# Column sums by one VectorE reduction and new shares of weight preparation in a two-layer conditional feed-forward kernel

## The chip, the cores and the metric

The kernel runs on one core of a Trainium2 chip. The metric is the device time of one execution in microseconds (us). A core has five engines with queues of their own that meet at semaphores: TensorE (PE, matrix products into PSUM), VectorE (DVE), ScalarE (ACT), GpSimd (POOL, which does not touch PSUM here) and SyncE (SP, which issues nearly all transfers). Each engine runs its instructions in the order in which they are written.

## The reference, cut to what matters

`x` is 32 x 64 x 1024 in fp32. Two layers follow one another, each with a residual:

```
x = x + ffn0(cond0(x));   x = x + ffn1(cond1(x))
cond(x)[b] = W[itok[b]]^T x[b]              # 64 x 64 matrix chosen by sample, contracts the channels
ffn0(y) = y @ (ternary(w) * scale) + b      # ternary(w) = 0 if |w| < 0.05 else sign(w)
          scale[o] = mean over k of |w[k, o]|
ffn1(y) = y @ dequant(q).T + bias + 4 * (y @ A.T) @ B.T
          dequant(q) = NF4_LEVELS[q] * q_scale (one scale for 64 values), A and B of rank 8
```

Everything is fp32. The scale of the first feed-forward is a column sum of absolute weights; it multiplies the product's columns.

## The kernel before, in words

**Tiles.** The 32 samples are 16 tiles (g = 0 to 15) of 128 rows and 1024 columns. Layer 1 takes the same tiles again as g = 16 to 31, in pairs. The 1024 output columns are two halves n of 512 (one PSUM bank each). TensorE's products use operands split in a high part (rounded to fp32r, by ScalarE) and a low part (the difference, by VectorE): `high_x` and `low_x` do this for the mixed input.

**Layer 0.** `mixed` or, from tile 4 (F = 4) on, `mixed_batches(g)` (L1159) applies the sample's 64 x 64 matrix on TensorE and leaves the transposed result in PSUM; ScalarE and VectorE split it. `mixed_batches(g)` waits for `low_x(g - 1)` (L1166), and the first of them, tile 4, waits for both `colscale` (L1164), since they read the same PSUM tile. `first` (tiles 0 to 3) and `main` (from tile 4 on) are sixteen matmuls each for one tile and one half against the ternary weights T0. VectorE's `leave_y(q)` (L936) multiplies the product by `col_scale` into `ys`, and GpSimd adds bias (`add_bias`, L600) and result (`result_half`, `result`) to x.

**Column sums.** ScalarE turns the sixteen weight blocks in `w_in` (8 row blocks k, two halves n) into absolute values (`absolute`, semaphore s_abs) after VectorE or ScalarE has made signs for `ternary`. GpSimd's `sums(n, 1, KB)` (L621) adds the eight blocks of a half in seven additions into `col_scale`; both halves are at the head of GpSimd's queue (L669, L670). `column_sums(n)` (L1273) adds over the partitions on TensorE with a matrix of ones; `column_sums(1)` stands in the middle of `first(1, 1)` (L1321). ScalarE's `colscale(n)` (L738) copies the sum out of PSUM divided by 1024. `leave_y(4)` is the first to need the second half.

**The weights of layer 1** are prepared during layer 0, in 16 pieces d of 128 x 512. For each piece ScalarE makes 8 lines of the integer levels (`lines`, L743), VectorE joins them by 6 maxima (`maxima`, L944), GpSimd takes the difference and scales it (`weight`), TensorE turns it and adds the LoRA part (`turn_w(d)`, L1289), and ScalarE and VectorE split it or make block sums of it (`high_w`, `low_w`, `keep_block`, `sums_with`), which depends on the rest of d by 4. At the end `high_sums` and `low_sums` split those sums.

**Stages.** The order is written out by stages m = 0 to 31. On VectorE and ScalarE stage m = 2g + n belongs to tile g and half n; for tiles 0 to 3 the eight stages lie behind the ternary weights, each with a share of the maxima and, at even m, one `leave_y(3 + g)`; from m = 8 on each starts with `leave_y(m - 1)`, then the operations on a piece turned in the stage before, then `low_x` of the next tile (even m), then the maxima. `low_x(4)` comes at the end of stage 6. `share(total, m)` (L196) says how much of a total is done before stage m: weight 3 for each of the first 8 stages, 10 for the next 21, the last three none. This gives 9 of the 96 maxima in the first eight stages, 4 or 5 in each of the others. `lines_by` makes the lines go some ahead, `ready_in(d)` (L212) is the stage that completes piece d's maxima, `turned_in(d)` (L216) is two later, but not before stage 8. ScalarE calls `colscale(1)` ahead of stage 2 (L874). SyncE loads the levels of a piece (`load_q`, L503, three buffers) when the lines of the piece three before are done, in the order of the loop at L560, ahead of spills and loads of x. In stages 29 to 31 `SPLIT_BY` (L185) puts 4, 5 and 1 of the late splits.

**Layer 1** works with pairs of tiles and seven products of half size for each pair; its right sides are the prepared weights.

Of the kernel before, what the change touches and what calls it, by code (L numbers as in the profile page):

```python
# [30 lines left out]
ALU = mybir.AluOpType  # L31
# [3 lines left out]
BANK = 512  # L35
# [66 lines left out]
def build(nc, x, itok, mix0, w0, b0, mix1, q_weight, q_scale, b1, lora_a, lora_b, out):  # L102
# [14 lines left out]
    B, C, T = x.shape  # L117
# [3 lines left out]
    NT = B * C // P  # L121
    KB = T // P
    NH = T // BANK
# [10 lines left out]
    F = 4  # L134
# [20 lines left out]
    ABS = ((2, 3, 0, 1, 5, 4, 7, 6), (0, 1, 2, 3, 4, 5, 6, 7))  # L155
# [36 lines left out]
    def stays(g):  # L192

        return SB <= g < SB + XS

    def share(total, m):  # L196


        m = min(m, NH * NT - 3)
        whole = 3 * NH * F + 10 * (NH * (NT - F) - 3)  # L200
        return total * (3 * min(m, NH * F) + 10 * max(0, m - NH * F)) // whole

    def lines_by(m):

# [7 lines left out]
    def ready_in(d):  # L212

        return next(m for m in range(NH * NT) if share(2 * NC * ND, m + 1) >= 2 * NC * (d + 1))

    def turned_in(d):  # L216

        return max(NH * F, ready_in(d) + 2)

    def blocks_before(d):  # L220

# [11 lines left out]
    with ExitStack() as ctx:  # L233
# [6 lines left out]
        def sem(name):  # L240
            return ctx.enter_context(nc.semaphore(name))
# [8 lines left out]
        col_scale = sb("col_scale", [P, T], F32)  # L250
# [42 lines left out]
        def w_raw(k, n):  # L293
            return w_in[:, k, n * BANK:(n + 1) * BANK]
# [100 lines left out]
        s_neg = sem("s_neg")  # L395
        s_T0 = sem("s_T0")
        s_sum = sem("s_sum")
        s_colsum = sem("s_colsum")
        s_colscale = sem("s_colscale")
        s_ah = sem("s_ah")  # L400
# [82 lines left out]
        def _(sp):  # L483
# [76 lines left out]
            for g in range(F, NT):  # L560
                load_mix(g + 3)
                for d in range(3, ND):
                    if d > 3 and ready_in(d - 3) // NH == g or d == 3 and g == F:
                        load_q(d)
                if g == F:
                    for t in range(F):
                        spill(t)
                else:
                    if g == NT - 1:
                        sp.wait_ge(s_xb, NT)  # L570
                        sp.dma_start(bias[:, :], b1.rearrange("(a f) -> a f", a=1).to_broadcast([P, T])
                                     ).then_inc(s_b1, 16)
                    if g - 1 < NT - XS:
                        spill(g - 1)
                    if g + 3 < NT:
                        load_x(g + 3)
# [21 lines left out]
        @block.gpsimd  # L598
        def _(pool):
            def add_bias(g):  # L600
                arrived(pool, g)
                pool.wait_ge(s_b1 if g >= NT else s_b0, 16)
                pool.wait_ge(s_xT, NH * (g + 1))
                pool.tensor_tensor(x_of(g), x_of(g), bias[:, :], ALU.add  # L604
                                   ).then_inc(s_xb, 1)

            def result_half(q):
                t, n = q % F, q // F
                pool.wait_ge(s_xb, t + 1)
                pool.wait_ge(s_ys, q + 1)  # L610
                pool.tensor_tensor(half(t, n), half(t, n), ys[:, t, :], ALU.add).then_inc(s_res0, 1)  # L611

            def result(g):
                pool.wait_ge(s_xb, g + 1)
                pool.wait_ge(s_ys, NH * (g + 1))
                at = NH * g % F
                pool.tensor_tensor(x_of(g), x_of(g),  # L617
                                   ys[:, at:at + NH, :].rearrange("p a f -> p (a f)"), ALU.add
                                   ).then_inc(s_res0, NH)

            def sums(n, start, stop):  # L621

                cols = slice(n * BANK, (n + 1) * BANK)
                for j in range(start, stop):
                    pool.wait_ge(s_abs, n * KB + j + 1)
                    if j == 1:
                        pool.tensor_tensor(col_scale[:, cols], w_raw(ABS[n][0], n), w_raw(ABS[n][1], n),
                                           ALU.add).then_inc(s_sum, 1)
                    else:
                        pool.wait_ge(s_sum, n * (KB - 1) + j - 1)  # L630
                        pool.tensor_tensor(col_scale[:, cols], col_scale[:, cols],  # L631
                                           w_raw(ABS[n][j], n), ALU.add).then_inc(s_sum, 1)

            def weight(d):
                k, n = PIECES[d]
                lev = side_p[:, d % SP, :]
                pool.wait_ge(s_max, 2 * NC * (d + 1))
                pool.tensor_tensor(lev, lev, side_n[:, :], ALU.subtract).then_inc(s_lev, 1)  # L638
                pool.wait_ge(s_lev, d + 1)
                sc = scales[:, n * HB:(n + 1) * HB, 2 * k:2 * k + 2].unsqueeze(3).to_broadcast(  # L640
                    [P, HB, 2, P // 2])
                lev4 = lev.rearrange("p (o g i) -> p o g i", o=HB, g=2)
                pool.tensor_tensor(lev4, lev4, sc, ALU.mult).then_inc(s_wn, 1)

            def weights_of(m):
                for d in range(ND):
                    if ready_in(d) == m:
                        weight(d)

            def low_side(p, i):  # L650

                o = (S1, S2, S3, S4)[i - 1]
                pool.wait_ge(s_sideh, NPR * p + o + 1)
                pool.tensor_tensor(side(o, 1).rearrange("p b c -> p (b c)"), plain(i),  # L654
                                   side(o, 0).rearrange("p b c -> p (b c)").bitcast(F32), ALU.subtract
                                   ).then_inc(s_Sl, 1)

            def add_sum(p, i):
                which, tile, n = SUMS[i]
                pool.wait_ge(s_xb, SB + 2 * p + tile + 1)  # L660
                pool.wait_ge(s_take, taken(p, 2 + which))
                t = half(SB + 2 * p + tile, n)
                pool.tensor_tensor(t, t, sum_of(which), ALU.add).then_inc(s_sum2, 1)  # L663

            pool.memset(ident[:, :], 0.0).then_inc(s_zero, 1)
            pool.wait_ge(s_zero, 1)
            pool.affine_select(out=ident[:, :], in_=ident[:, :], compare_op=ALU.not_equal, fill=1.0,
                               base=0, pattern=[[-1, P]], channel_multiplier=1).then_inc(s_ident, 1)
            sums(0, 1, KB)  # L669
            sums(1, 1, KB)  # L670
            add_bias(0)
            result_half(0)
            add_bias(1)
            result_half(1)
            pool.wait_ge(s_scales, 16)
            add_bias(2)
            result_half(2)
            for m in range(NH * F - 3):
                weights_of(m)
            add_bias(3)  # L680
            result_half(3)
            result_half(F)
            add_bias(F)
            result_half(F + 1)
            for m in range(NH * F - 3, NH * F + 1):
                weights_of(m)
            result_half(F + 2)
            for g in range(F, SB):
                if g == F:
                    result_half(F + 3)  # L690
                else:
                    result(g - 1)
                if g > F:
                    weights_of(NH * g)
                add_bias(g + 1)
                weights_of(NH * g + 1)
            for i in range(1, 5):
                low_side(0, i)
            result(NT - 1)
            add_bias(SB + 1)  # L700
            for p in range(NP):
                for i in range(len(SUMS)):
                    add_sum(p, i)
                if p + 1 < NP:
                    add_bias(SB + 2 * p + 2)
                    low_side(p + 1, 1)
                    low_side(p + 1, 2)
                    add_bias(SB + 2 * p + 3)
                    low_side(p + 1, 3)
                    low_side(p + 1, 4)  # L710

        @block.scalar
        def _(act):
# [157 lines left out]
            act.wait_ge(s_ain, 64)  # L871
            act.activation(loraA[:, :], a_raw, ACT.Copy).then_inc(s_ah, 1)
            for g in range(SB):
                if g == 1:  # L874
                    colscale(1)
                for m in (NH * g, NH * g + 1):
                    for d in range(ND):
# [31 lines left out]
        def _(dve):  # L909
# [169 lines left out]
            leave_y(1)  # L1079
            for k in range(4, KB):  # L1080
                ternary(1, k)
            dve.wait_ge(s_ah, 1)
            dve.tensor_tensor(loraA[64:P, :], a_raw[64:P, :], loraA[64:P, :].bitcast(F32),
                              ALU.subtract).then_inc(s_al, 1)
# [46 lines left out]
        def _(pe):  # L1131
# [139 lines left out]
                mm.then_inc(s_prod, 1)  # L1271

            def column_sums(n):  # L1273
                pe.wait_ge(s_sum, (n + 1) * (KB - 1))
                pe.wait_ge(s_fill, 3)
                pe.wait_ge(s_hl, NH * 3)
                pe.matmul(flat(n), ones[:, :], col_scale[:, n * BANK:(n + 1) * BANK],
                          start=True, stop=True).then_inc(s_colsum, 1)
# [88 lines left out]
```

## Time and profile before

| | us |
|---|---|
| median of 3 runs | 343.64 |
| lowest and highest | 343.38, 344.93 |
| profiled execution, its time | 344.56 |
| its span | 342.5 |
| PE busy | 332.4 (97%) |
| POOL busy | 245.0 (72%) |
| DVE busy | 236.0 (69%) |
| ACT busy | 164.5 (48%) |

The span runs from the first to the last instruction; the time of the execution has 2.1 us more around it. The clock granted to TensorE was 0.999 of full speed. A row of the timeline gives the start, the duration, the engine and the line of the kernel, the instruction, the tile written and the tile read, their shapes, how many rows were merged, and in brackets how long the engine was idle before it and what ended that.

### The profile page before, as it was taken

The numbers are of one execution on the slowest core, as the hardware profiler recorded it, in microseconds if no ns is written. First come the engines' busy times: TensorE is split into PE (matmuls) and PEld (weight loads), VectorE is DVE, ScalarE is ACT, GpSimd is POOL, SyncE is SP. The second block draws the span as 40 slices with busy tenths as digits, with TensorE's granted clock in tenths as the row PEclk, the third lists the DMA queues.
The fourth block names the chain that finished last, engine by engine and source line by source line (L and its number), as shares of the span: only waits on it lengthen the run. The fifth ranks groups of instructions, "written<-read, shape, count | busy, mean of one in ns | idle before, by whom it ended". The sixth has DMA issues, their size and how long they took to land.

```text
span 342.5 us, 8187 instructions
## 1 busy us (share of the span) xinstructions
PE 332.4 (97%) x3142; PEld 271.4 (79%) x3142; DVE 236.0 (69%) x356; ACT 164.5 (48%) x300; POOL 245.0 (72%) x160
## 2 busy tenths in 40 slices
PE   7999999989999999999799999999999999999996
PEld 6868778778888778887678888888888888888884
DVE  7787567899999999999999736346263462624623
ACT  1799357877897787788171403214032140411400
POOL 0298999998896896986578966766467664677642
PEclk9999999999999999999999999999999999999999
DMA  6894511644354245300100151412513124150302
GB/s 229 291 341 132 201 33 33 271 168 159 118 167 162 93 157 177 141 10 13 55 2 3 65 189 63 150 44 74 181 65 131 63 84 169 67 169 23 124 31 92
DMA packets 25800, 40.60 MB, mean 119 GB/s; under 512 B 7810, under 2 KB 16002, under 8 KB 25762
## 3 DMA queue, kind: packets, MB, share of 16 engines
q1 hardware_dynamic: 25090, 39.48, 33.3%
q10 hardware_dynamic: 672, 0.61, 0.5%
q8 instruction: 25, 0.41, 0.5%
q14 instruction: 13, 0.11, 0.1%
HBM read 25.40 MB, written 14.68 MB: 117 GB/s over the span
## 4 chain that ended last, share of the span: by engine, by line
PE 51%; DVE 20%; POOL 12%; issue 8%; ACT 4%; DMA 1%; SPq 1%; DVEq 0%; POOLq 0%; ACTq 0%
PE acc L1268 45%; POOL col_scale L631 4%; DVE hl L914 3%; DVE ys L941 3%; POOL x_first L604 3%; PE spare L1154 2%; PE xT L1154 2%; POOL x_first L611 2%; DVE side_n L953 2%; ACT spare L762 2%; DVE W L988 2%; DMA w_in<-in_L_ffn_w 1%; POOL side_p L638 1%; DVE side_p L953 1%; DVE side_n L956 1%
## 5 line engine op out<-in xcount | busy, mean ns | idle before, releaser
L1268 PE MATMUL acc<-W,hh 128*128 128x512 f32 x256 | 81.4, 389 | 0.0
L1228 PE MATMUL acc<-T,hh 128*128 128x512 f32 x192 | 76.5, 398 | 0.0
L1228 PE MATMUL acc<-T,hl 128*128 128x512 f32 x192 | 75.0, 391 | 0.0
L604 POOL TENSOR_TENSOR X<-X,bias 128x1024 f32<-128x1024 f32 x28 | 68.1, 2432 | 0.0
L762 ACT ACTIVATE spare<-q_raw 128x512 f32<-128x512 int32 x96 | 56.1, 599 | 20.2 <-DVE side_n L953 5.0
L1040 DVE TENSOR_TENSOR X<-X,acc 128x512 f32<-128x512 f32 x48 | 32.9, 685 | 36.7 <-PE acc L1268 28.9
L1268 PEld LDWEIGHTS acc<-W,hh 128*128 128x128 f32 x256 | 48.0, 188 | 10.0
L663 POOL TENSOR_TENSOR X<-X,ys 128x512 f32<-128x512 f32 x24 | 30.5, 1299 | 34.1 <-DVE ys L1029 34.1
L1268 PE MATMUL acc<-W,hl 128*128 128x512 f32 x128 | 49.8, 389 | 0.0
L797 ACT ACTIVATE hh<-xT 128x512 fp32r<-128x512 f32 x16 | 8.7, 595 | 77.6 <-PE xT L1154 77.6
L1228 PEld LDWEIGHTS acc<-T,hh 128*128 128x128 f32 x192 | 36.0, 188 | 8.0
L1228 PEld LDWEIGHTS acc<-T,hl 128*128 128x128 f32 x192 | 36.1, 188 | 7.3
L1029 DVE TENSOR_TENSOR ys<-acc,ys 128x512 f32<-128x512 f32 x16 | 11.0, 690 | 34.2 <-PE acc L1268 33.3
L617 POOL TENSOR_TENSOR X<-X,ys 128x1024 f32<-128x1024 f32 x12 | 29.3, 2438 | 2.8 <-DVE ys L941 2.7
L638 POOL TENSOR_TENSOR side_p<-side_p,side_n 128x512 f32<-128x512 f32 x16 | 20.8, 1299 | 13.4 <-DVE side_n L959 13.4
L1268 PEld LDWEIGHTS acc<-W,hl 128*128 128x128 f32 x128 | 24.0, 188 | 5.0
L654 POOL TENSOR_TENSOR side_S<-plain_sums,side_S 128x512 fp32r<-128x512 f32 x8 | 10.4, 1302 | 23.0 <-ACT side_S L814 23.0
L941 DVE TENSOR_TENSOR ys<-acc,col_scale 128x512 f32<-128x512 f32 x32 | 21.8, 683 | 3.7 <-POOL x_first L611 3.7
L1268 PE MATMUL acc<-W 128*128 128x512 f32 x96 | 24.0, 399 | 0.0
L1268 PE MATMUL acc<-W,side_S 128*128 128x512 f32 x96 | 23.2, 390 | 0.0
L1268 PE MATMUL acc<-W_T,W 128*128 128x512 f32 x96 | 23.1, 389 | 0.0
L654 POOL TENSOR_TENSOR hl<-plain_sums,hh 128x512 fp32r<-128x512 f32 x16 | 21.6, 1353 | 0.0
(98 smaller groups left out, 606.5 us busy)
## 6 DMA issues: line engine op xcount, KB each, us to landing
out<-X SPq DMA_DIRECT2D x22, 512.0 KB, 3.1
X<-in_x SPq DMA_DIRECT2D x12, 512.0 KB, 3.4
X<-out SPq DMA_DIRECT2D x12, 512.0 KB, 3.8
q_raw<-in_L_ffn_q_weight SPq DMA_DIRECT2D x16, 256.0 KB, 2.9
w_in<-in_L_ffn_w SPq DMA_DIRECT2D x14, 256.0 KB, 6.8
x_first<-in_x SPq DMA_DIRECT2D x4, 512.0 KB, 5.1
out<-x_first SPq DMA_DIRECT2D x4, 512.0 KB, 4.6
out<-X SPq DMA_DIRECT2D x4, 256.0 KB, 2.0
```

The source lines that it names most:

```text
L604: pool.tensor_tensor(x_of(g), x_of(g), bias[:, :], ALU.add).then_inc(s_xb, 1)
L617: pool.tensor_tensor(x_of(g), x_of(g), ys[:, at:at + NH, :].rearrange("p a f -> p (a f)"), ALU.add).then_inc(s_res0, NH)
L631: pool.tensor_tensor(col_scale[:, cols], col_scale[:, cols], w_raw(ABS[n][j], n), ALU.add).then_inc(s_sum, 1)
L638: pool.tensor_tensor(lev, lev, side_n[:, :], ALU.subtract).then_inc(s_lev, 1)
L654: pool.tensor_tensor(side(o, 1).rearrange("p b c -> p (b c)"), plain(i), side(o, 0).rearrange("p b c -> p (b c)").bitcast(F32), ALU.subtra ...
L663: pool.tensor_tensor(t, t, sum_of(which), ALU.add).then_inc(s_sum2, 1)
L762: act.activation(dst, q_raw[:, d % QS, :, :].rearrange("p o i -> p (o i)"), ACT.Copy, scale=slope, bias=offset).then_inc(s_line, 1)
L941: dve.tensor_tensor(ys[:, q % F, :], acc[:, bank_of(q), :], col_scale[:, n * BANK:(n + 1) * BANK], ALU.mult).then_inc(s_ys, 1)
L1040: dve.tensor_tensor(t, t, bank, ALU.add).then_inc(s_take, 1)
L1154: mm = pe.matmul(turned(g, h)[c * C:(c + 1) * C, k, rows], x_of(g)[rows, at:at + C], mix[rows, g % NM, rows], start=True, stop=True)
L1228: mm = pe.matmul(acc[:, bank_of(q), :], a[:, k, :], T0[:, n, k, :], start=(k == 0 and j == 0), stop=(k == KB - 1 and j == 1))
L1268: mm = pe.matmul(acc[:, bank, :], a[:, k, :], w1(part, c, k), start=(k == 0 and j == 0), stop=(k == HB - 1 and j == len(terms) - 1))
```

## The change

It touches the column sums of the second half and the spread of the weight preparation over the stages.

- The second half's eight absolute blocks are summed by one `tensor_reduce` on VectorE, behind the last `ternary(1, k)` and ahead of the loraA difference, in place of seven additions on GpSimd. `column_sums(1)` waits for it (s_reduce).
- `share` uses a list of weights: 5 for each of the first eight stages, 10 for the next 18, 6 for the last three. The maxima of the stages become 2 in each of the first eight (16 in all), 4 in each of stages 8 to 25, then 3, 2 and 3. They were 1, 1, 1, 1, 2, 1, 1, 1 and then 4, with 5 in stages 9, 19 and 28.
- `turned_in(d)` is at least stage 8 + d. The stages in which pieces 0 to 15 are turned become 8, 9, 10, 11, 13, 14, 16, 17, 19, 20, 22, 23, 25, 26, 28, 30. They were 8, 10, 11, 13, 14, 16, 17, 19, 20, 22, 23, 25, 26, 28, 29, 30.
- ScalarE calls `colscale(1)` ahead of stage 4 instead of stage 2.
- On GpSimd `add_bias(2)` and `add_bias(3)` come ahead of the results that stood before them.
- `load_q(d)` follows the new stages; for tile 4's turn of SyncE's loop it is pieces 3 to 6.

```
+    SHARES = [5] * (NH * F) + [10] * 18 + [6] * 3
     def share(total, m):
-        m = min(m, NH * NT - 3)
-        whole = 3 * NH * F + 10 * (NH * (NT - F) - 3)
-        return total * (3 * min(m, NH * F) + 10 * max(0, m - NH * F)) // whole
+        return total * sum(SHARES[:m]) // sum(SHARES)
...
     def turned_in(d):
-        return max(NH * F, ready_in(d) + 2)
+        return max(NH * F + d, ready_in(d) + 2)
...
                 for d in range(3, ND):
-                    if d > 3 and ready_in(d - 3) // NH == g or d == 3 and g == F:
+                    if max(F, ready_in(d - 3) // NH) == g:
                         load_q(d)
...
-            sums(0, 1, KB)
-            sums(1, 1, KB)
+            sums()
             add_bias(0)
             result_half(0)
             add_bias(1)
             result_half(1)
+            add_bias(2)
             pool.wait_ge(s_scales, 16)
-            add_bias(2)
+            add_bias(3)
             result_half(2)
             for m in range(NH * F - 3):
                 weights_of(m)
-            add_bias(3)
             result_half(3)
...
             for g in range(SB):
-                if g == 1:
+                if g == 2:
                     colscale(1)
...
             for k in range(4, KB):
                 ternary(1, k)
+            dve.wait_ge(s_abs, NH * KB)
+            dve.tensor_reduce(col_scale[:, BANK:T], w_in[:, :, BANK:T].rearrange("p k f -> p f k"),
+                              mybir.AxisListType.X, ALU.add).then_inc(s_reduce, 1)
...
             def column_sums(n):
-                pe.wait_ge(s_sum, (n + 1) * (KB - 1))
+                if n == 0:
+                    pe.wait_ge(s_sum, KB - 1)
+                else:
+                    pe.wait_ge(s_reduce, 1)
```

## Rows read from the trace of the kernel before

**Rows 1.** The page's first part: busy us, share of the span, instructions.

```profile
PE 332.4 (97%) x3142; PEld 271.4 (79%) x3142; DVE 236.0 (69%) x356; ACT 164.5 (48%) x300; POOL 245.0 (72%) x160
```

**Rows 2.** Timeline of PE, opening: start, us, line, operation, tiles, idle before.

```profile
38.52 1.02 PE L1277 MATMUL xT<-col_scale,ones 128*128 128x512 f32 x2
...
44.96 1.16 PE L1172 MATMUL xT<-mix,X 64*64 64x64 f32 x64
46.05 3.92 PE L1216 MATMUL acc<-T,h 128*128 128x512 f32 x16
49.90 1.16 PE L1172 MATMUL xT<-mix,X 64*64 64x64 f32 x64
```

**Rows 3.** Timeline of PE, from tile 5 on: mixings and the last piece.

```profile
70.21 1.16 PE L1172 MATMUL xT<-mix,X 64*64 64x64 f32 x64
...
79.46 1.16 PE L1172 MATMUL xT<-mix,X 64*64 64x64 f32 x64
...
88.75 1.16 PE L1172 MATMUL xT<-mix,X 64*64 64x64 f32 x64
...
98.78 1.16 PE L1172 MATMUL xT<-mix,X 64*64 64x64 f32 x64
...
157.63 1.48 PE L1154 MATMUL xT<-mix,X 64*64 64x64 f32 x64
164.82 0.63 PE L1296 MATMUL acc<-ident,side_p 128*128 128x128 f32 x4 [1.86 <-DVE W_sums L978]
...
165.61 1.48 PE L1154 MATMUL spare<-mix,X 64*64 64x64 f32 x64
```

**Rows 4.** Groups of instructions: the piece turned; busy us, mean ns, idle before.

```profile
L1296 PE MATMUL acc<-ident,side_p 128*128 128x128 f32 x64 | 9.7, 274 | 3.5 <-DVE W_sums L978 1.9 <-DVE W_sums L974 1.3 <-DVE W_sums L981 0.3
```

**Rows 5.** Busy time by stretch: PE, PEld, DVE, ACT, POOL, clock, DMA.

```profile
70.00:155.00 85.00, 84.23 (x916) 68.28 (x915) 80.10 (x128) 68.50 (x129) 70.42 (x42) 1.00 0.40 135
```

**Rows 6.** Timeline of DVE, opening and the late splits.

```profile
32.19 0.69 DVE L932 SCALAR_TENSOR_TENSOR T<-w_in,spare 128x512 fp32r<-128x512 f32 x1 [0.46 <-ACT w_in L736]
33.14 1.25 DVE L1083 TENSOR_TENSOR loraA<-a_in,loraA 64x1024 fp32r<-64x1024 f32 x1 [0.26 <-ACT loraA L872]
34.43 0.69 DVE L941 TENSOR_TENSOR ys<-acc,col_scale 128x512 f32<-128x512 f32 x1
35.03 0.68 DVE L953 SCALAR_TENSOR_TENSOR side_p<-side_p,spare 128x512 f32<-128x512 f32 x1
...
40.70 0.69 DVE L959 TENSOR_TENSOR side_p<-side_p,spare 128x512 f32<-128x512 f32 x1 [3.80 <-ACT spare L762]
...
41.91 0.68 DVE L953 SCALAR_TENSOR_TENSOR side_n<-side_n,spare 128x512 f32<-128x512 f32 x1
42.69 0.69 DVE L956 SCALAR_TENSOR_TENSOR side_n<-side_n,spare 128x512 f32<-128x512 f32 x1
...
46.81 1.29 DVE L914 TENSOR_TENSOR hl<-xT,hh 128x512 fp32r<-128x512 f32 x2 [0.65 <-ACT hh L720]
...
52.95 0.69 DVE L941 TENSOR_TENSOR ys<-acc,col_scale 128x512 f32<-128x512 f32 x1 [3.66 <-POOL x_first L611]
...
156.62 5.66 DVE L988 TENSOR_TENSOR W<-W_sums,W 128x512 fp32r<-128x512 f32 x4
```

**Rows 7.** Timeline of ACT: the second half's scale.

```profile
39.58 0.60 ACT L740 ACTIVATE col_scale<-xT 128x512 f32<-128x512 f32 x1 [4.94 <-PE xT L1277]
```

**Rows 8.** Timeline of POOL: six of the second half's adds.

```profile
26.25 9.30 POOL L631 TENSOR_TENSOR col_scale<-col_scale,w_in 128x512 f32<-128x512 f32 x6
```

**Rows 9.** Groups of VectorE instructions near to the new one; busy us, mean ns.

```profile
L941 DVE TENSOR_TENSOR ys<-acc,col_scale 128x512 f32<-128x512 f32 x32 | 21.8, 683 | 3.7 <-POOL x_first L611 3.7
...
L1083 DVE TENSOR_TENSOR loraA<-a_in,loraA 64x1024 fp32r<-64x1024 f32 x1 | 1.3, 1252 | 0.3 <-ACT loraA L872 0.3
...
L1044 DVE MEMSET b_wide<- 128x1024 f32 x1 | 0.9, 912 | 0.2 <-issue 0.2
...
L1058 DVE CAST loraB<-acc 128x512 fp32r<-128x512 f32 x2 | 2.1, 1117 | 1.2 <-PE acc L1284 1.2
```

More of the change, by code:

```diff
@@ L397, in build @@
         s_sum = sem("s_sum")
+        s_reduce = sem("s_reduce")
         s_colsum = sem("s_colsum")
@@ L619, in result, with sums @@
                                    ).then_inc(s_res0, NH)
[L621 to L625, printed above, removed]
+            def sums():
+                cols = slice(0, BANK)
+                for j in range(1, KB):
+                    pool.wait_ge(s_abs, j + 1)
                     if j == 1:
-                        pool.tensor_tensor(col_scale[:, cols], w_raw(ABS[n][0], n), w_raw(ABS[n][1], n),
+                        pool.tensor_tensor(col_scale[:, cols], w_raw(ABS[0][0], 0), w_raw(ABS[0][1], 0),
                                            ALU.add).then_inc(s_sum, 1)
                     else:
-                        pool.wait_ge(s_sum, n * (KB - 1) + j - 1)
+                        pool.wait_ge(s_sum, j - 1)
                         pool.tensor_tensor(col_scale[:, cols], col_scale[:, cols],
-                                           w_raw(ABS[n][j], n), ALU.add).then_inc(s_sum, 1)
+                                           w_raw(ABS[0][j], 0), ALU.add).then_inc(s_sum, 1)
             def weight(d):
```

## The prediction

> **What bounds the kernel now.** The engine shares come first [rows 1]: TensorE is busy for 332.4 of 342.5 us, so the time is TensorE's work plus the few places where it waits, and another engine counts only where it makes TensorE wait. Next I read TensorE in order of time through layer 0. In the opening [rows 2] the column sums of the second half start at 38.52, the mixing of tile 4 at 44.96 and that of tile 5 at 49.90 with no wait between. From tile 5 on [rows 3] a tile with one turned weight piece takes 9.25 us (70.21 to 79.46) and one with two 10.03 (88.75 to 98.78). The eleven tiles from 49.90 to 157.63 have fifteen pieces: 11 x 8.47 + 15 x 0.78 = 104.9 us, and take 107.7, so 2.8 us are lost. From 157.63 to 165.61 there is one mixing (1.48), one `main` (3.7) and one piece (0.8), 6.0 of 8.0 us: 2.0 more. Of these 4.8 us the rows show 3.5 as waits before a piece is turned, ended by VectorE's weight sums [rows 4]; the largest, 1.86, is at 164.82 [rows 3]. The rest are short waits of the queue and matmuls that are slower just behind one. The stretch behind 185 us is not touched by the change.
>
> From 70 to 155 us VectorE is as full as TensorE (80.1 of 85 us [rows 5], and what is missing is the start of one operation behind another). But in the opening it idles [rows 6]: 3.80 us at 40.70, because ScalarE, standing in `colscale(1)` until 39.58 [rows 7], made no lines, 0.65 at 46.81, and 3.66 at 52.95, because GpSimd was late with `result_half`.
>
> **The change part by part.** *The adds that go.* Seven GpSimd adds go, six of which take 9.30 us from 26.25 [rows 8]. TensorE did not wait for them: the sums were out at 35.55 and the matmul came at 38.52 [rows 2]. What follows on GpSimd starts up to 10 us earlier, once the bias has landed, and the 3.66 us of VectorE at 52.95 go, as the result it waited for is then early. None of this is on TensorE's path by itself.
>
> *The reduction.* The trace has no such instruction. It reads 8 x 512 elements per partition, neighbours of the sum 4 KB apart, at one output in eight reads. From below: a memset of 1024 elements, which reads nothing, takes 0.912 us [rows 9], so 4096 are put at no less than 3.65. Packed operations that read: 1.252 us for 1024 against 0.683 for 512, a slope of 1.11 ns, gives 0.683 + 3584 x 1.11 ns = 4.7 us. The only VectorE operation here with far apart elements is the cast at L1058, which writes with a step of 32 bytes: 1.117 us where a packed one takes 0.683, so 0.85 ns more for each element [rows 9]. With that for the reads: 4.7 + 4096 x 0.85 ns = 8.1 us. From above: 8 x 1.117 = 8.9 us. I take 8.1, since far apart elements are what the two have in common and the only ones measured cost it, and keep 3.65 and 8.9 for the range.
>
> The Trainium skill is of two minds on this. Its page "SBUF — State Buffer" (section "Door 1: The DMA port swizzle") says that full rate wants at least two accesses in each 16-byte line and that a new line at every access costs extra; the cast bears it out for writes, no row here shows it for reads. Its page "VectorE: DVE Perf Modes" (section "Mode 1× (REGULAR) — the baseline") says that the plain mode gives one result a cycle whatever the stride; with its formula of (N + 151) cycles at 0.96 GHz that would be an estimated 4.4 us. The second is the first rival below.
>
> *The path through the opening.* The last `ternary` starts at 32.19 [rows 6] and the next instruction can follow 0.60 later, so the reduction runs 32.8 to 40.9. `column_sums(1)` on TensorE, in order at 38.52, waits for it: 2.4 us. VectorE's queue behind the reduction is the loraA difference (1.29), `leave_y(2)` (0.6), then maxima and `leave_y` in order; one follows another after 0.60, or 0.78 where it needs the one before [rows 6]. The new shares put two maxima in each of the first eight stages (16 in all) where there were nine. ScalarE now takes `colscale(1)` only after the lines of four stages, eleven of them, and the eleventh must wait for the sixth maximum, which is done at 47.7 (42.2 for `leave_y(2)`, then two maxima, `leave_y(3)`, four maxima). A line and `colscale(1)`, 0.6 each, end at 48.9. `mixed_batches(4)` waits for that: 48.9 for 44.96, 3.9 late in all. `leave_y(4)` starts at 48.9 too.
>
> *Tile 5.* `mixed_batches(5)` waits for `low_x(4)`. Before, eight maxima stood in front of it on VectorE, and it was done at 48.1, 1.8 us before TensorE came for it [rows 2, 6]. Now 14 do: from 48.9 come `leave_y(4)`, four maxima, `leave_y(5)`, four maxima, then the two `low_x`: 6 x 0.60 + 4 x 0.78 + 1.29 = 8.0 us (ScalarE's copies for it, some 0.6 us each, are hidden: they can start 6.0 in, when the line behind the twelfth maximum is made). It is done at 56.9. TensorE comes at 48.9 + 4.94 = 53.8 and waits 3.1. So `mixed_batches(5)` is at 56.9 for 49.90: **7.0 us late**. What the six early maxima and the reduction fill of VectorE's idle time is in this sum already.
>
> *What comes back.* From stage 26 on the maxima are 3, 2 and 3 for 4, 4 and 5, and with stage 24 and the piece operations VectorE has seven operations fewer (some 4.6 us) before the late `low_sums`, which took 5.66 us in one block at 156.62 [rows 6] and stood in front of the two sums that TensorE waited for at 164.82. Piece 14 is turned at stage 28 instead of 29, so its sums now come ahead of that block. The 2.0 us there and the wait of that kind before 157.63 go. In the middle a close pair remains: old, pieces with rest 1 and 2 were turned in neighbouring stages (10/11, 16/17, 22/23, 28/29) with one sum between; new, rest 2 and 3 are (10/11, 16/17, 22/23), with three VectorE operations between. For the first pair, counted from `mixed_batches(5)`: TensorE is there after 1.1 + 3.75 + 0.75 + 3.7 + 0.75 + 1.1 + 3.7 + 0.75 + 3.7 = 19.3 us; VectorE has two `leave_y` and two maxima (2.5), `low_x(5)` (to 3.7), four maxima (6.7), `leave_y`, `low_w` and four maxima (11.2), `leave_y`, a sum and `low_x(6)` (14.2), four maxima (17.2), and `leave_y` with the three (19.7). I leave 0.4 us for this and 0.4 for the other two, where the two engines go at one rate. Of 4.8 us lost, **4.0 come back**; the bounds are none and all.
>
> *Other edits.* `add_bias` and the `s_scales` wait swap on GpSimd, with slack. SyncE's `load_q` moves with the shares, and its fourth now stands before the spills of tiles 0 to 3 and waits for 32 lines; `load_x(8)` now stands behind the lines of stage 11, a whole tile before its own is mixed. Nothing on the path: the stretch of TensorE between covers it, and if it didn't, the transfer would be late once, by the part that sticks out, some 1 us.
>
> *Sum.* 7.0 - 4.0 = +3.0 us. The profiled execution has a span of 342.5 us and a time of 344.56, 0.9 above the median; against itself it becomes 347.6, and the median of 343.64 becomes **346.6 us**.
>
> **Rivals.** *A: the reduction runs at the packed rate, 4.7 us.* It ends at 37.5, before TensorE comes to the column sums. All steps are 3.4 us earlier: `low_x(4)` at 53.5, 3.6 late, 4.0 back: -0.4, so 343.2 us. For it: it is one input stream, and no read in the trace shows a stride cost. Against it: the cast.
>
> *B: faster.* The reduction goes at the rate of a memset (3.65) and every later wait vanishes: `low_x(4)` at 52.5, 2.6 late, 4.8 back, -2.2, so 341.4 us. It is one mechanism, VectorE's idle 8.1 us of the opening used for work that the late stages then lack, and it decides from where `low_x(4)` comes before about 53.0 (reduction under 4.2 us). Against it: 14 maxima are in front.
>
> *C: the shares bring nothing back.* If the late waits come from the order of the pieces and `low_sums` rather than from the number of maxima, the 7.0 us stay whole: 350.6 us (347.2 with the packed rate). For it: TensorE and VectorE go at one rate, so a stage cannot catch up. Against it: the two sums do move ahead of the block.
>
> **How the numbers follow.** Forecast 0.55, A 0.28, B 0.08, C 0.09. Within 0.5% (1.7 us) is about what a measurement of this kernel can tell from no change. The forecast's own range is 345.4 to 348.2 (reduction 7.3 to 8.9, 3.2 to 4.3 back); nearly all of it is slower. A lies within 0.5% in three of four cases and splits the rest. So faster 0.12, same 0.24, slower 0.64. The range reaches down into A's lower side and up to the forecast's upper end: 342.2 to 348.3, leaving out B and most of C.
>
> **What would show it.** The first row to look at is the reduction's duration: 8 us or 4.5. Then `column_sums(1)` (40.9 or 38.5), `mixed_batches(4)` (48.9 or 45.5) and `mixed_batches(5)` (56.9 or 53.5); the wait before the second mixing names `low_x(4)` on VectorE. Then the distance from `mixed_batches(5)` to the first `mixed_alone`, 107.7 before and some 105.7 after, and no wait before the piece after it. I am wrong in the opening if the maxima in front of `low_x(4)` cost less than 0.60 each or ScalarE does not hold `colscale(1)` back; wrong in the middle if that distance does not shrink.

## The result and the profile after

| | us |
|---|---|
| before, median of 4 runs | 343.8 (343.38 to 344.93) |
| after, median of 4 runs | 349.53 (347.33 to 351.10) |
| ratio, 95% interval | 1.015 (1.0096 to 1.0204) |
| profiled execution after: time, span, granted clock | 347.33, 345.3, 0.995 |

The change makes the kernel slower by 1.5%. The forecast was 346.6 with a range to 348.3. The profiled execution is the fastest of the four; the others have spans of 347.5, 347.5 and 349.3 at clocks of 0.995, 0.994 and 0.990. The kernel before had 0.999 in its profile. Beside the experiments it ran 79 times: 58 executions had 0.998 to 1.000, and 21 had 0.994 or 0.995 and were 0.9 us longer in the mean. So there are two questions: where the profiled execution's +2.8 us of span come from, and what the others lose besides.

The page's first part, after:

```profile
PE 331.6 (96%) x3142; PEld 270.7 (78%) x3142; DVE 244.3 (71%) x357; ACT 164.8 (48%) x300; POOL 234.8 (68%) x153
```

VectorE has 8.3 us more and GpSimd 10.2 less [rows 1]: the one instruction more, the seven less. Below, "mixing 4" and "mixing 5" are `mixed_batches(4)` and `mixed_batches(5)`. Timeline of VectorE: the reduction, `leave_y(4)` and `low_x(4)`.

```profile
32.38 7.53 DVE L1084 TENSOR_REDUCE col_scale<-w_in 128x512 f32<-128x4096 f32 x1
...
48.30 0.69 DVE L942 TENSOR_TENSOR ys<-acc,col_scale 128x512 f32<-128x512 f32 x1 [1.24 <-ACT col_scale L741]
...
55.27 1.28 DVE L915 TENSOR_TENSOR hl<-xT,hh 128x512 fp32r<-128x512 f32 x2
```

Timeline of TensorE: the rows that answer to [rows 2, 3], L1284 the column sums, L1176 a mixing, L1220 `first`, L1158 `mixed_alone`, L1272 a product of layer 1.

```profile
39.96 1.12 PE L1284 MATMUL xT<-col_scale,ones 128*128 128x512 f32 x2 [1.73 <-DVE col_scale L1084]
48.35 1.16 PE L1176 MATMUL xT<-mix,X 64*64 64x64 f32 x64 [1.80 <-ACT col_scale L741]
49.44 5.53 PE L1220 MATMUL acc<-T,h 128*128 128x512 f32 x16
56.70 1.16 PE L1176 MATMUL xT<-mix,X 64*64 64x64 f32 x64 [1.72 <-DVE hl L915]
61.56 0.60 PE L1303 MATMUL acc<-ident,side_p 128*128 128x128 f32 x4
...
161.63 1.48 PE L1158 MATMUL xT<-mix,X 64*64 64x64 f32 x64
166.85 0.60 PE L1303 MATMUL acc<-ident,side_p 128*128 128x128 f32 x4
167.61 1.48 PE L1158 MATMUL spare<-mix,X 64*64 64x64 f32 x64
...
179.13 3.01 PE L1272 MATMUL acc<-W,side_S 128*128 128x512 f32 x12 [0.73 <-DVE ys L942]
187.51 0.69 PE L1158 MATMUL xT<-mix,X 64*64 64x64 f32 x32
```

Three waits stand in the opening where there were none. Mixing 5 is at 56.70 for 49.90, 6.8 us late: the three waits are 5.25 us, and `first(3, 1)` between the last two takes 5.53 us where it took 3.92 [rows 2]. From there to the first `mixed_alone` it is 104.93 us for 107.73, and on to the second 5.98 for 7.98: all 4.8 us of [rows 3, 4] are gone. From there to the next pair it is 19.90 for 19.11, a new loss of 0.8. Sum: 6.8 - 2.8 - 2.0 + 0.8 = +2.8 us, the difference of the spans.

The new 0.8 us: product 3 waits for `leave_y(31)`, behind five `low_sums` that take 6.60 us where they took 4.90. First the kernel after (VectorE, then GpSimd), then the kernel before. (The bracket at 165.93 names a transfer, but the addition starts 0.2 us behind the end of VectorE's `leave_y`, as the one at 163.05 does.)

```profile
166.88 6.60 DVE L989 TENSOR_TENSOR W<-W_sums,W 128x512 fp32r<-128x512 f32 x5
165.93 2.38 POOL L619 TENSOR_TENSOR X<-X,ys 128x1024 f32<-128x1024 f32 x1 [3.12 <-DMA bias<-in_L_ffn_bias]
168.28 2.84 POOL L606 TENSOR_TENSOR X<-X,bias 128x1024 f32<-128x1024 f32 x1
```

```profile
165.79 4.90 DVE L988 TENSOR_TENSOR W<-W_sums,W 128x512 fp32r<-128x512 f32 x5
163.05 2.36 POOL L617 TENSOR_TENSOR X<-X,ys 128x1024 f32<-128x1024 f32 x1 [1.93 <-DVE ys L941]
165.37 2.37 POOL L604 TENSOR_TENSOR X<-X,bias 128x1024 f32<-128x1024 f32 x1
```

After, one GpSimd addition from SBUF begins inside the block and runs along with it; before, the last one ends 1.95 us into it. That fits the Trainium skill, page "SBUF — State Buffer", section "Who interferes with whom": a VectorE instruction with two inputs in SBUF contends with GpSimd reads, a `tensor_reduce` does not. On the `tensor_reduce` the trace agrees: GpSimd's result addition at 32.96, beside the reduction, took 1.30 us as elsewhere. The 0.8 us come with the new shares and not with the reduction: shares_only, which has no reduction, has the block of 6.60 us and a wait of 0.73 there, and reduce_only, with the old shares, has 4.88 and no wait. That the second GpSimd addition is what lengthens the block was not tested by itself; `three_adds` below shows the two engines' additions slowed side by side.

### The profile page after: what moved, and what is told of

Its sections match the earlier page's. It is cut to its first block, busy times and chain, and to the rows that moved or that the text cites. A ratio compares the mean times of both kernels' runs of the same rounds, so it can differ in the third digit from the quotient of the medians.

```text
span 345.3 us, 8175 instructions
## 1 busy us (share of the span) xinstructions
PE 331.6 (96%) x3142; PEld 270.7 (78%) x3142; DVE 244.3 (71%) x357; ACT 164.8 (48%) x300; POOL 234.8 (68%) x153
## 4 chain that ended last, share of the span: by engine, by line
PE 77%; DVE 8%; issue 6%; ACT 6%; SPq 1%; DMA 1%; DVEq 0%; ACTq 0%
PE acc L1272 43%; PE acc L1232 23%; PE xT L1176 3%; PE xT L1158 2%; PE acc L1303 2%; PE spare L1158 2%; ACT spare L731 2%; ACT w_in L737 2%; DVE W L989 1%; DMA w_in<-in_L_ffn_w 1%; PE acc L1305 1%; DVE ys L942 1%; ACT spare L763 1%; DVE T L933 1%; DVE side_p L954 1%
## 5 line engine op out<-in xcount | busy, mean ns | idle before, releaser
L1272 PE MATMUL acc<-W,hh 128*128 128x512 f32 x256 | 81.4, 389 | 0.0
L1272 PEld LDWEIGHTS acc<-W,hh 128*128 128x128 f32 x256 | 48.1, 188 | 10.0
L1272 PE MATMUL acc<-W,hl 128*128 128x512 f32 x128 | 49.8, 389 | 0.0
L1272 PEld LDWEIGHTS acc<-W,hl 128*128 128x128 f32 x128 | 24.0, 188 | 5.0
L1272 PE MATMUL acc<-W 128*128 128x512 f32 x96 | 24.0, 399 | 0.0
L1272 PE MATMUL acc<-W,side_S 128*128 128x512 f32 x96 | 23.2, 390 | 0.7 <-DVE ys L942 0.7
L1272 PE MATMUL acc<-W_T,W 128*128 128x512 f32 x96 | 23.1, 389 | 0.0
L1272 PEld LDWEIGHTS acc<-W,side_S 128*128 128x128 f32 x96 | 17.9, 188 | 4.8 <-DVE ys L942 1.1
```

The source lines that it names most:

```text
L1272: mm = pe.matmul(acc[:, bank, :], a[:, k, :], w1(part, c, k), start=(k == 0 and j == 0), stop=(k == HB - 1 and j == len(terms) - 1))
```

## Experiments

Theories: **T**, the account above. **K**, the waits that TensorE now has in the opening make its granted clock fall from 2.4 to 1.2 GHz behind them; where that stretch lies ahead of another wait it is hidden, otherwise it adds to the time. The rivals are in the expectations. The kernel before ran again beside each group of experiments (14 or 17 executions, medians 343.9 to 344.6), and the ratios are to those.

| kernel | median us (lowest to highest) | ratio to before, 95% interval | clock of the profile |
|---|---|---|---|
| after_again | 348.98 (347.76 to 350.44) | 1.0119 (1.0089 to 1.0150) | 0.990 |
| shares_only | 349.00 (348.78 to 349.82) | 1.0140 (1.0112 to 1.0167) | 0.990 |
| reduce_only | 345.52 (344.66 to 346.61) | 1.0031 (1.0015 to 1.0048) | 0.995 |
| packed_reads | 346.56 (346.54 to 347.75) | 1.0069 (1.0046 to 1.0092) | 0.995 |
| filled_waits | 347.33 (346.95 to 347.63) | 1.0081 (1.0053 to 1.0110) | 0.999 |
| early_three | 346.98 (346.60 to 347.43) | 1.0072 (1.0051 to 1.0094) | 0.994 |
| colscale_early | 348.09 (347.86 to 348.71) | 1.0110 (1.0080 to 1.0140) | 0.990 |
| weight0_early | 345.89 (345.22 to 346.14) | 1.0040 (1.0026 to 1.0054) | 1.000 |
| balanced | 345.41 (344.76 to 346.51) | 1.0035 (1.0021 to 1.0050) | 1.000 |
| three_adds | 349.91 (349.48 to 352.32) | 1.0189 (1.0152 to 1.0226) | 0.989 |
| balanced_second | 344.07 (341.97 to 344.64) | 0.9991 (0.9973 to 1.0009) | 0.995 |
| balanced_third | 345.42 (342.84 to 346.85) | 1.0024 (1.0003 to 1.0045) | 0.995 |

**after_again**: no edit.

> The changed kernel once more, for its spread and a second profile. Theory T (the opening): mixed_batches(5) is late by some 7 us and 4 to 5 us come back later, so +3 us; that alone gives 346.7 to 347.3 in every execution. Theory K (the clock): the changed kernel's new waits of TensorE in the opening make the granted clock fall to half for some us behind them, and where that stretch lies beside TensorE's next wait it is hidden (as in the profile, +3), elsewhere it costs 2 us and more: executions differ, between 347 and 351 us, with the mean granted clock at 0.990 to 0.995, while the kernel before stays at 343.4 to 345 and 0.999.

Its profile is of its longest execution (span 348.4 for 345.3). Mixing 5 is at 56.46, as in the other profile, but the piece after it is turned 7.62 us later for 4.86. TensorE, and the granted clock by stretch (third column from the right):

```profile
56.46 1.99 PE L1176 MATMUL xT<-mix,X 64*64 64x64 f32 x64 [3.32 <-DVE hl L915]
64.08 0.60 PE L1303 MATMUL acc<-ident,side_p 128*128 128x128 f32 x4
...
56.00:58.00 2.00, 1.54 (x57) 1.57 (x61) 1.73 (x4) 1.12 (x2) 1.64 (x2) 0.50 0.00 0
58.00:60.00 2.00, 2.00 (x23) 1.59 (x16) 1.93 (x4) 1.50 (x4) 0.00 (x0) 0.50 0.00 0
60.00:62.00 2.00, 2.00 (x7) 1.52 (x6) 1.90 (x4) 1.81 (x5) 0.11 (x1) 0.50 0.12 35
```

In the first profile the clock fell a wait earlier (the same view of the kernel after):

```profile
50.00:52.00 2.00, 2.00 (x6) 1.62 (x5) 1.78 (x4) 1.80 (x4) 2.00 (x3) 0.50 0.00 0
52.00:54.00 2.00, 2.00 (x8) 1.55 (x7) 1.90 (x4) 1.76 (x4) 2.00 (x1) 0.76 0.11 33
...
56.00:58.00 2.00, 1.30 (x65) 1.27 (x66) 1.74 (x3) 1.24 (x4) 1.87 (x2) 1.00 0.00 0
```

There it lengthened `first(3, 1)` from 3.92 to 5.53 us, and as TensorE had to wait for `low_x(4)` until 56.7 anyway, that cost nothing. It is the same program with the same `low_x(4)` to wait for, and the piece is 2.5 us later by the clock alone. The other 0.6 us between the two spans lie behind 190 us and were not traced to a cause.

**filled_waits**:

```
+            keep_busy(flat(1), 7)        # 7 matmuls T0 x T0, nobody reads them
             column_sums(1)
...
+            pe.wait_ge(s_ys, 4)
+            keep_busy(acc[:, 3, :], 7)
             mixed_batches(F)
             first(3, 1, 0)
             first(3, 1, 1)
             pe.wait_ge(s_al, 1)
+            pe.wait_ge(s_ys, 5)
+            keep_busy(acc[:, 0, :], 14)
```

> The changed kernel with 7, 7 and 14 matmuls of 0.23 us, whose results nobody reads, put where TensorE waits in the opening (ahead of the second column sums, of mixing 4 and of mixing 5). Theory K (the clock falls behind an idle TensorE): the granted clock stays at 1.0 throughout, a piece is turned 4.9 us after mixing 5 in each execution, the time is 347.0 to 347.8 with a spread under 1.5 us, 1.5 to 2 us below the changed kernel's median, although TensorE does more. Rival R (the clock falls in these executions for another reason, or the spread comes from elsewhere): the median stays at 349 or goes up by what the matmuls overrun the waits.

As K says: TensorE gets 28 matmuls more, mixing 5 stays where it was, the clock of the four executions is 0.998 to 1.000, the spread 0.7 us, and the median 1.7 to 2.2 us below the changed kernel's two (1.3 to 2.4 by the ratios). Of the changed kernel's eight executions only the profiled one, 347.33, is as short as these four (346.95 to 347.63). What is left, 2.9 us above the kernel before beside it, is T's sum.

```profile
56.72 1.16 PE L1176 MATMUL xT<-mix,X 64*64 64x64 f32 x64 [0.17 <-DVE hl L915]
40.00:60.00 20.00, 19.60 (x201) 15.55 (x202) 17.08 (x27) 14.05 (x26) 12.08 (x9) 1.00 0.10 28
```

**packed_reads**:

```
-w_in[:, :, BANK:T].rearrange("p k f -> p f k")
+w_in[:, 0:HB, :].rearrange("p k (f j) -> p (k f) j", j=KB)
```

> The changed kernel with the reduction reading 4096 elements in a row (blocks 0 to 3, eight neighbours for each sum) instead of elements 4 KB apart; so the second half's scale is that of other elements. If the stride is what costs, the reduction takes 4.4 to 4.7 us instead of 7.5, the column sums no longer wait, low_x(4) is 3 us earlier and mixed_batches(5) near 53.6; theory T then gives 343.5 to 344.5 us. If the reduction is slow by itself, it takes 7.5 us again and the time is that of the changed kernel. Theory K: with one wait fewer in the opening the spread of the executions shrinks.

The reduction takes 4.41 us for as many elements, 4096, so the stride of 4 KB costs 3.1 us, 0.76 ns an element; no other stride was run. TensorE no longer waits for the sums, and mixing 5 is 2.7 us earlier. It still waits 3.32 there and the clock falls behind that: the piece is turned 6.47 us after mixing 5 for 4.86, so 1.6 of the 2.6 us by which 346.6 misses 344 are the clock's.

```profile
32.33 4.41 DVE L1084 TENSOR_REDUCE col_scale<-w_in 128x512 f32<-128x4096 f32 x1
```

```profile
54.03 1.16 PE L1176 MATMUL xT<-mix,X 64*64 64x64 f32 x64 [3.32 <-DVE hl L915]
```

**reduce_only**: the old shares (`[3] * 8 + [10] * 21`), stages, colscale(1) ahead of stage 2 and GpSimd's old order, with the reduction.

> The kernel before with the reduction alone on VectorE; shares, stages, the place of colscale(1) and GpSimd's order of biases as before. Theory T: the column sums are 1.5 us late (40.0 for 38.5), low_x(4) comes near 50 with eight maxima in front, mixed_batches(5) is near 51.4, and the later waits (4.8 us) stay, so +1.5 us: 345.2 us. Theory K adds what the clock takes behind the wait for the column sums: up to 349. Rival S: if only the shares were at fault, this is 343.8.

Mixing 5 is at 51.27, without a wait, and the late waits are back: 345.5, 0.9 above the kernel before beside it, where T said +1.5. The clock falls at the late wait, which the kernel before has too [rows 3], where the clock stayed at 1.00 in its profile:

```profile
165.75 0.63 PE L1303 MATMUL acc<-ident,side_p 128*128 128x128 f32 x4 [1.85 <-DVE W_sums L979]
165.00:190.00 25.00, 24.16 (x277) 19.88 (x278) 24.16 (x30) 9.37 (x18) 17.61 (x10) 0.93 0.01 2
```

**shares_only**: the reverse, the changed kernel with GpSimd's seven adds.

> The changed kernel with the second half summed by GpSimd as before (seven adds); shares, turned stages, ScalarE's later colscale(1) and the order of SyncE stay. Theory T: without the reduction (7.5 us) VectorE gets through its 14 maxima in time, leave_y(4) near 40.2 and low_x(4) near 48.2, so mixed_batches(5) stays at 49.9 and all 4.8 us of the later waits come back: 339 us (338.5 to 340.5), no fall of the clock. Rival S (the larger early shares are what is too much): low_x(4) is still late by 2 us or more, 341 to 343 us. Rival P: GpSimd, again late with the results, gives part of the later waits back: 341 to 342.

T's number was wrong by 10 us. `leave_y(4)` came at 40.2 as expected, but the tenth of the maxima then had to wait for 7.4 us: ScalarE's line of piece 1 waited for GpSimd's subtraction on piece 0, which stood behind four biases and three results.

```profile
49.34 0.63 ACT L763 ACTIVATE side_n<-q_raw 128x512 f32<-128x512 int32 x1 [7.20 <-POOL side_p L639]
42.07 4.75 POOL L605 TENSOR_TENSOR x_first<-x_first,bias 128x1024 f32<-128x1024 f32 x2
46.76 1.31 POOL L612 TENSOR_TENSOR x_first<-x_first,ys 128x512 f32<-128x512 f32 x1
48.00 1.31 POOL L639 TENSOR_TENSOR side_p<-side_p,side_n 128x512 f32<-128x512 f32 x1
55.90 1.98 PE L1173 MATMUL xT<-mix,X 64*64 64x64 f32 x64 [6.83 <-DVE hl L915]
```

So with the larger early shares GpSimd must either be rid of the second half's sums, as in the change, or take piece 0 earlier, as the last four kernels do: balanced_second keeps the sums on GpSimd and has mixing 5 at 49.69.

**early_three**: `SHARES = [3] * 8 + [10] * 18 + [6] * 3`.

> The changed kernel with weight 3 instead of 5 for the first eight stages (10 maxima there instead of 16; some 4.3 in the middle stages), all else kept: the reduction, the light last stages, the late colscale(1). Theory T2 (the reduction of 7.5 us and the six early maxima together overfill VectorE ahead of low_x(4); each alone is mostly absorbed): mixing 5 is near 51.4, with no wait in front of it, the later waits are gone as in the changed kernel, 341.5 to 342.5 us, clock at 1.0. Rival: the light stages can't be had without the early shares; then the later waits return in part, 343 to 345.

A miss, on both counts. Mixing 5 is at 53.05 and not at 51.4. In this profile the clock fell behind the 2.39 us wait for the sums, so TensorE came there just as `low_x(4)` was done; but `low_x(4)` is done only at 52.90 whatever the clock, as VectorE waited 1.24 us for the late `colscale(1)` at `leave_y(4)`. So the fall cost little here, and the four executions with a clock of 1.000 are at 346.6 to 347.2 beside 347.43. And the maxima saved in the opening return in the middle stages (4.3 each), and so do the waits. VectorE's `low_x(4)`, then TensorE:

```profile
51.62 1.28 DVE L915 TENSOR_TENSOR hl<-xT,hh 128x512 fp32r<-128x512 f32 x2
```

```profile
91.23 0.63 PE L1303 MATMUL acc<-ident,side_p 128*128 128x128 f32 x4 [0.31 <-DVE W L966]
121.09 0.63 PE L1303 MATMUL acc<-ident,side_p 128*128 128x128 f32 x4 [1.17 <-DVE W L966]
141.68 0.63 PE L1303 MATMUL acc<-ident,side_p 128*128 128x128 f32 x4 [1.15 <-DVE W_sums L982]
```

The rival holds: light last stages need the early shares. Its 343 to 345 us were too low, as it too had the opening at 51.4.

**colscale_early**: `if g == 1: colscale(1)`.

> The changed kernel with ScalarE's colscale(1) ahead of stage 2 again. Theory T2: mixing 4 no longer waits for it (46.4 instead of 48.2), but mixing 5 waits for low_x(4) all the same, which comes at 56.5 less at most 1.2 us (VectorE's wait of 1.24 at leave_y(4)): mixing 5 at 55.3 to 56.5, with a longer wait in front of it, and by theory K a longer stretch of half clock behind it. 348 to 350 us. Rival: if the place of colscale(1) is what delays the opening, mixing 5 is near 52 and the time near 344.

Mixing 4 is at 45.84 without a wait; mixing 5 waits 3.91 us and is at 54.77, 1.7 us earlier than in after_again: 1.24 are VectorE's wait at `leave_y(4)`, which is gone, and 0.4 an earlier start of the reduction (31.73 for 32.14). The clock falls behind it. 348.1 us: `low_x(4)` sets the opening.

**three_adds**: the reduction as three packed additions (4, 2, 1 blocks).

> The changed kernel with the reduction replaced by three packed VectorE additions (four blocks to four, two to two, one to one: 2048, 1024 and 512 elements). If the stride is what makes the reduction slow, the three take 2.3 + 1.2 + 0.7 = 4.2 us, or up to 5.5 where a GpSimd addition holds the port that two inputs from SBUF need, and the kernel goes as packed_reads did: 346 to 347 us. If VectorE's additions are slowed more by GpSimd, 348 or more.

They run from 31.65 to 39.5, as long as the reduction, where 4.2 us were expected of them alone. GpSimd's additions beside them are slowed as well: a result takes 3.22 us for 1.3. VectorE, then GpSimd:

```profile
31.65 5.07 DVE L1087 TENSOR_TENSOR w_in<-w_in 128x2048 f32<-128x2048 f32 x2
36.76 2.73 DVE L1087 TENSOR_TENSOR col_scale<-w_in 128x512 f32<-128x512 f32 x1
32.42 3.22 POOL L613 TENSOR_TENSOR x_first<-x_first,ys 128x512 f32<-128x512 f32 x1
35.60 6.09 POOL L606 TENSOR_TENSOR x_first<-x_first,bias 128x1024 f32<-128x1024 f32 x2
```

This is the last rival of the expectation, 348 us or more: packed additions with two inputs are no way round the stride while GpSimd adds beside them. The clock fell twice in this profile, behind waits of 2.04 and 2.22 us.

**Attempts at a faster kernel.** weight0_early is shares_only with GpSimd's `weight(0)` behind result 0 and `weight(1)` behind result 4.

> The kernel with new shares and GpSimd's seven adds (shares_only), but with GpSimd's work on piece 0 put behind the first result instead of behind the third, since there ScalarE's lines of piece 1 waited 7.2 us for it. Theory Q (in shares_only GpSimd's queue, not the number of maxima, made low_x(4) late): low_x(4) is done near 48, mixing 5 at 49 to 50 without a wait, all later waits are gone, clock at 1.0: 339.5 to 341 us, faster than both kernels. Rival S (14 maxima are too many in any case): low_x(4) near 52, 343 us. Rival: GpSimd is late at leave_y(7) and mixing 6 waits, 342.

Mixing 5 waits only 1.18 us and all waits from 75 to 165 are gone, but the first piece waits 2.59 for `leave_y(7)`, and two later ones 0.65 and 0.52. At 345.9 theory Q is right on what held shares_only up and wrong on the amount by 5 us. balanced adds `SHARES = [9] * 8 + [20] * 18 + [18, 14, 14]`.

> The column sums with GpSimd as before; GpSimd's work on piece 0 behind the first result, on piece 1 behind the fifth; colscale(1) ahead of stage 4; shares 9 for the first eight stages, 20 for the next 18, then 18, 14, 14 (14 maxima in the first eight stages, 12 of them ahead of low_x(4), exactly 4 in each middle stage, 4, 3, 3 at the end; piece 14 turned at stage 28). Theory Q (the opening is bounded by VectorE's and GpSimd's queues together, the late waits by the maxima in stages 26 to 28): low_x(4) is done by 49.6, mixing 5 comes without a wait, GpSimd has leave_y(7) released by 53.6, just before the first piece is turned; 2 us and more of the later waits are gone: 340.5 to 342.5 us, clock 1.0, faster than before. Rival: GpSimd still holds leave_y(7) or piece 1 back, and the opening loses 2 to 3 us: 343 to 344.5.

The rival: GpSimd stood waiting for piece 0's maxima, result 1 came late, and VectorE waited for it 4.22 us. balanced_second puts `weight(0)` behind result 1 and `weight(1)` behind result 3.

> The kernel balanced with GpSimd's work on piece 0 one result later (behind result 1) and on piece 1 behind result 3. In balanced GpSimd stood 2.71 us waiting for piece 0's maxima and so held back result 1, for which leave_y(5) waited 4.22 us. Theory Q: that wait goes, low_x(4) is done near 48, mixing 5 comes without a wait at 4.94 us behind mixing 4, and GpSimd releases leave_y(7) near 52.3: 2.5 us of balanced's opening and 0.5 to 1 us of its waits at 62 and 83 come back, 341.5 to 343 us, faster than the kernel before by 0.4 to 0.8%. Rival: piece 0 or 1 is now late for ScalarE's lines, and the opening still loses 1.5 us or more: 344 to 345.5.

The opening is now free of waits (mixing 5 at 49.69), one large wait is left at 80.98, and the clock falls behind it. TensorE, and two stretches:

```profile
49.69 1.16 PE L1172 MATMUL xT<-mix,X 64*64 64x64 f32 x64
80.98 0.63 PE L1296 MATMUL acc<-ident,side_p 128*128 128x128 f32 x4 [2.68 <-DVE W_sums L981]
40.00:62.00 22.00, 22.00 (x277) 17.80 (x276) 16.72 (x26) 14.11 (x27) 21.53 (x15) 1.00 0.24 84
62.00:85.00 23.00, 20.32 (x206) 16.35 (x205) 20.91 (x34) 17.33 (x34) 21.86 (x15) 0.93 0.43 152
```

Its twelve executions: four at 341.97 to 342.65, all with clock 1.000, the other eight at 343.6 to 344.6 with 0.989 to 0.995. The median is that of the kernel before. balanced_third moves `weight(2)` ahead of `add_bias(4)`.

> The kernel balanced_second with GpSimd's work on piece 2 ahead of add_bias(4) instead of behind it and result 5. In balanced_second VectorE waited 1.51 us at 62.4 for lines that needed piece 2, and TensorE later 2.68 us at 80.98 for a weight sum of VectorE, behind which the granted clock fell. Theory: with piece 2 earlier by some 2 us that wait shrinks to under 1.2 us, the clock stays at 1.0 in nearly all executions, and the time is 340.5 to 342.3 us, faster than the kernel before by 0.5 to 1%. Rival: the wait at 81 comes from the neighbouring stages 12 and 13 of pieces 3 and 4 (one main between, three VectorE operations), not from the lines; then it stays above 2 us and the time at 342 to 344.5, with executions in two groups some 2 us apart by the clock.

The wait grew to 3.25 us: its rival holds as far as the wait stays. But the edit also moved a wait elsewhere: VectorE now stands 2.08 us at 63.26 for a result of GpSimd, which comes behind piece 2, and 1.26 for a line at 72.76. So which of the two made the wait at 81 was not settled. No version beat the kernel before.

## Why the prediction was wrong, and where it was right

- *The reduction*, 8.1 us taken from the cast's stride [rows 9]: 7.53. The ends 3.65 and 8.9 held; the packed rate, 4.7 by slope, is 4.41. The Trainium skill's line rule ("SBUF — State Buffer", section "Door 1: The DMA port swizzle") is borne out for reads, as far as one stride can show it; the constant rate whatever the stride ("VectorE: DVE Perf Modes", section "Mode 1× (REGULAR) — the baseline") is not, and holds only packed.
- *The opening*: the column sums at 39.96 (40.9 forecast), mixing 4 at 48.35 (48.9), mixing 5 at 56.70 (56.9), each behind the wait that was named. Right, with two errors that balance: the reduction ended 1.0 us earlier than forecast, and the chain behind it was 0.8 slower. The wait in front of mixing 5 was 3.32 in after_again (3.1 forecast) and 1.72 in the first profile, where the slower clock took the other 1.6 us.
- *What comes back*: 4.8 us for 4.0. The three close pairs of stages, for which I left 0.8, cost nothing.
- *Missed on the way*: the 0.8 us behind the five `low_sums`; with it the sum for the profiled execution, +2.8 for +3.0, was right by the luck of two small errors.
- **The step that failed** is the sum itself: "7.0 - 4.0 = +3.0 us" set the price of each new TensorE wait at its own length, and so put the clock at nothing. The added waits have a second price, the clock behind them. In the profiled execution it was hidden, in after_again's it was not (2.8 us): filled_waits, without it, is at 347.33 with a ratio of 1.0081, the changed kernel at 349.53 and 348.98 with 1.0150 and 1.0119. So about 2 us, 1.3 to 2.4 by the ratios, are the clock's, 2.9 are T's, which was forecast, and the rest of the 5.7 us is scatter: the first four executions of the kernel before had a median of 343.8, the larger sets later up to 344.6. The prediction had the clock in no row and no rival.
- *Rivals*: A's condition (packed rate) failed, and packed_reads shows that even then the kernel is slower, by 1.9 us where A had it faster by 0.4; 1.6 of this is the clock. B and C did not happen. My account of the seven adds was incomplete: "none of this is on TensorE's path by itself" was true for the kernel before, but shares_only shows that with 14 maxima in front of `low_x(4)` those adds would have been on it, unless GpSimd takes piece 0 earlier.

## What to carry to other kernels

Where TensorE is the bound, count the waits that a change adds to it and not only their sum: behind waits of 1.8 to 6.8 us the granted clock fell to half for some 3 to 7 us in most profiles here and not in all, and one profile can show the lucky execution, so look at the clock of several. What a fall costs depends on whether TensorE would have waited next anyway. Before moving work to the front of an in-order queue, find the operation that the bounding engine needs next from that queue, and count what now stands ahead of it. Moving adds from one engine to another is worth their length on the second engine with its access pattern, not on the first.

## What the runs showed of the hardware

- VectorE's `tensor_reduce` in fp32: 4.41 us for 4096 elements in a row, 7.49 to 7.62 with elements 4 KB apart (six profiles).
- The granted clock halved behind TensorE waits of 3.3 us and more in every profile that had one in the opening (after_again 3.32, packed_reads 3.32, colscale_early 3.91, shares_only 6.83), and behind waits of 1.7 to 2.7 us in some (1.80 in the kernel after, 1.85 in reduce_only, 2.04 and 2.22 in three_adds, 2.39 in early_three, 2.68 in balanced_second) and not in others (1.79 in after_again, 1.86 in the profile before, 2.50 in balanced, 2.59 in weight0_early). What decides between them was not found. Behind mixing 5, where nothing hid it, the fall made the matmuls up to the first piece 1.6 us (packed_reads) to 2.8 us (after_again) longer.
- Cheap matmuls that nobody reads, 28 of them in three waits, kept the clock at 0.998 to 1.000 in four executions of four and took 1.7 to 2.2 us off the changed kernel's medians.
- Three packed VectorE additions with two inputs in SBUF took 7.8 us beside GpSimd's additions, 5.07 and 2.73, and GpSimd's result took 3.22 us for 1.3 (three_adds).
